# Layer norms and head norms: the power -1/2 on GpSimd in place of a root on ScalarE and a reciprocal on VectorE

## The chip, the cores and the metric

The kernel runs on one core of one Trainium2 chip. The time is device microseconds from the start to the end of one execution. The engines of a core work side by side and wait for each other by semaphores: TensorE (PE in the rows) multiplies, VectorE (DVE) and ScalarE (ACT) read and write both memories of the core, GpSimd (POOL) only the large one, and SyncE (SP) issues transfers. Each engine executes its own instructions strictly in order: one that waits holds everything behind it.

## What is computed

Four layers of a small transformer, each an attention and a feed-forward part, on 2048 rows of 128 features. Each of the eight parts is added to its input and normalised:

```python
def _layernorm(x, axis=-1, eps=1e-05):
    m = jnp.mean(x, axis=axis, keepdims=True)
    v = jnp.var(x, axis=axis, keepdims=True)
    return (x - m) / jnp.sqrt(v + eps)

x = _layernorm(x + _L0_attn_ref(x, ...), axis=-1)
x = _layernorm(x + _L0_ffn_ref(x, ...), axis=-1)
...
x = _layernorm(x + _L3_ffn_ref(x, ...), axis=-1)
```

The feed-forward part of layer 0 is itself a small transformer of depth 2 with local attention. It has a layer norm of its own and an L2 norm of each query and key head of 64 features:

```python
def l2norm(t):
    return t / jnp.clip(jnp.linalg.norm(t, axis=-1, keepdims=True), 1e-12)
q = l2norm(q) * qs
k = l2norm(k) * ksc
q, k = rotary_xpos(q, k)      # then scores (8 * q) k, softmax, values
...
h = (h - mu) / jnp.sqrt(var + 1e-05) * lg + lb
```

## The kernel before

The rows are held as four batches b of 512: 128 partitions by four quarters of 128 features. The parts of the reference are eight stages after a short Begin: Paired (attention of layer 0), Local (its feed-forward), Shifted (attention 1), Experts (feed-forward 1), Paired again (attention 2), Ternary (feed-forward 2), Clipped (attention 3) and Routed (feed-forward 3). Each stage is a class. Its `plan` is one list of steps, such as ("scores", 7) or ("fin", b), and `sequence` strings the plans together, with the head of one stage among the tail steps of the one before. Every engine goes through that one list and executes its own share of each step (`on_tensor`, `on_vector`, `on_scalar`, `on_gpsimd`, `on_sync`). So the order on an engine is the order of the list, whatever is ready. A stage's `parts` says how many signals each engine gives in a step; an engine without an entry does nothing in it.

The step "fin" of a batch is its layer norm. `normalise_vector` (L328 to L346) runs on VectorE: four bn_stats (L331), four bn_aggr (L336), the addition of epsilon to the four variances of each row (L339), then a wait for ScalarE, the reciprocal (L341) and four subtract-and-multiply operations (L344) that write the new activations XK. `normalise_scalar` (L349 to L351) is ScalarE's share, the root of a 128x4 tile. Shifted has the same as steps "ln" (L1190 to L1197, root L1317) and "fin" (L1202, L1205). Local has it twice, as "ln" and as "fin". Of such norms there are 40. Behind "fin" comes "turnx": TensorE transposes the new activations and ScalarE copies them to XT.

ScalarE's functions lie in tables, and the compiler puts an ACT_TABLE_LOAD in front of an activation whose function is not in the table that is loaded. In the attention stages ScalarE takes exponentials of scores (L739 in Paired, L1298 in Shifted), in Experts SiLU (L2070), in Local exponentials and GELU in turn. TensorE writes scores into the banks that those exponentials and VectorE's row maxima (L684 in Paired, L1147 and L1151 in Shifted) read.

Local's head norm is the step "norm", one for each of eight groups of four iterations. VectorE sums the squares (L1709), ScalarE takes the root of a 128x64 tile (L1811), VectorE takes the maximum with 1e-12 (L1714), the reciprocal (L1716) and eight times the query half (L1718). GpSimd then scales queries and keys in four "scale" steps (L1861, 128x1024 each) and has "sum" steps (L1856) between them. ScalarE's copies for the token shift (L1781, L1782) feed TensorE's products L1593.

In Routed a batch has nine "hidden" steps (L2725 and L2727 on TensorE, SiLU L2843, product L2815 on VectorE). GpSimd multiplies eight of the nine results by the routing weights ("scale", L2854), and "outward" is 72 matmuls (L2737) that wait for the batch's last scaling, followed by the addition (L2820) and "fin". The plan runs as follows:

```python
for n in range(9 * NB):
    b, c = n // 9, n % 9
    plan.append(("hidden", n))
    ...
    if b and c < 8:
        plan.append(("scale", b - 1, c))
    if n in (21, 29, 35):
        b = (21, 29, 35).index(n)
        plan += [("outward", b), ("fin", b)]
b = NB - 1
return plan + [("scale", b, c) for c in range(8)] + [("outward", b), ("fin", b)]
```

Of the kernel before, what the change touches and what calls it, by code (L numbers as in the profile page):

```python
# [41 lines left out]
def _tables():  # L42
# [17 lines left out]
    c["rqa"], c["rqb"], c["rka"], c["rkb"] = tile(ca * s2), tile(sa * s2), tile(ca / s2), tile(sa / s2)  # L60
# [267 lines left out]
def normalise_vector(e, w, vs, ss, key, y, st, dst):  # L328
# [532 lines left out]
class Shifted:  # L861
# [12 lines left out]
    def __init__(self, C):  # L874
# [2187 lines left out]
```

## Time and profile before

| | |
|---|---|
| runs | 2252.64 us median of 3 (2249.35 to 2254.05) |
| profiled execution, first to last instruction | 2256.5 us |
| TensorE busy | 2015.2 us, 89% |
| VectorE busy | 1461.1 us, 65% |
| ScalarE busy | 1170.8 us, 52% |
| GpSimd busy | 811.4 us, 36% |

The profiled execution has a span 3.9 us above the median of the runs. A timeline row gives the start and the length of an instruction, or of a run of equal ones, and in brackets how long the engine stood before it and what ended that. Groups give a mean over all instructions of a line and shape. A row of windows gives the busy time of each engine in a stretch and, as PEclk, the granted clock of TensorE as a share of full speed. TensorE being the busiest engine does not make it the bound everywhere: each stretch has to be read by what TensorE waits for in it.

### The profile page before, as it was taken

The page shows a single profiled execution, that of the slowest core. Times are in us where ns is not written, and L with a number is a line of the kernel's source. Part 1 is how long each engine was busy: PE and PEld are TensorE (multiplying, and loading weights), DVE is VectorE, ACT ScalarE, POOL GpSimd, SP SyncE. Part 2 cuts the span into 40 slices and gives each one's busy share as a digit, 9 for nine tenths or more (in the row PEclk, how much of TensorE's full clock was granted, in tenths as well). Part 3 has the DMA queues.
Part 4 walks back from the last instruction along what each step waited for, and adds up shares of the span by engine and source line. Part 5 has one row for each costly group of instructions (what it writes and reads, how often), then busy time and mean ns, then how long its engine had stood idle before and what let it go on. Part 6 is the DMA issues. An engine that isn't in the chain of part 4 may idle for free.

```text
span 2256.5 us, 44998 instructions
## 1 busy us (share of the span) xinstructions
PE 2015.2 (89%) x17759; PEld 1190.8 (53%) x17759; DVE 1461.1 (65%) x2920; ACT 1170.8 (52%) x1950; POOL 811.4 (36%) x1153
## 2 busy tenths in 40 slices
PE   7887789999878999998999889999799898999888
PEld 3343456666644454544665344444565665666446
DVE  5775677888778777773555776121677676767474
ACT  2565456656623454555332467332576675757432
POOL 4554333433127748342001321000545344453042
PEclk8999899999998999999999899999999999999999
DMA  3430111111234434210201220000465564655161
GB/s 124 140 111 2 25 32 27 30 32 28 64 108 128 131 91 138 75 34 14 91 1 62 84 84 19 33 0 1 156 208 173 176 207 133 207 175 168 50 127 45
DMA packets 183993, 199.15 MB, mean 88 GB/s; under 512 B 55922, under 2 KB 152486, under 8 KB 179302
## 3 DMA queue, kind: packets, MB, share of 16 engines
q1 hardware_dynamic: 183782, 196.27, 29.6%
q8 instruction: 141, 2.31, 0.4%
q14 instruction: 70, 0.57, 0.1%
HBM read 93.53 MB, written 92.08 MB: 82 GB/s over the span
## 4 chain that ended last, share of the span: by engine, by line
PE 35%; DVE 7%; ACT 6%; issue 2%; DMA 2%; POOL 1%; SPq 1%; DVEq 0%; ACTq 0%; POOLq 0%
PE PS L2134 5%; PE PS L357 4%; PE PS L2383 3%; PE PS L2399 3%; PE PS L2371 3%; PE PS L1985 3%; ACT AR L2543 3%; PE PS L1972 2%; PE PS L1975 2%; PE PS L2737 2%; PE PS L617 1%; PE PS L2725 1%; PE PS L2727 1%; PE PS L596 1%; PE PS L2143 1%
## 5 line engine op out<-in xcount | busy, mean ns | idle before, releaser
L1298 ACT ACTIVATE AR<-PS 128x1024 f32<-128x1024 f32 x160 | 162.5, 1023 | 122.5 <-PE PS L1047 121.6
L739 ACT ACTIVATE AR<-PS 128x1024 f32<-128x1024 f32 x160 | 162.6, 1024 | 92.4 <-PE PS L548 44.5
L1151 DVE TENSOR_REDUCE AR<-PS 128x2 f32<-128x768 f32 (+1 forms) x192 | 159.9, 864 | 52.1 <-PE PS L1026 29.9
L2599 POOL TENSOR_TENSOR RA<-AR,RA 128x288 f32<-128x288 f32 x128 | 88.1, 697 | 275.3 <-DVE RA L2475 141.0
L2543 ACT ACTIVATE AR<-PS,AR 128x512 f32<-128x512 f32 x256 | 173.7, 686 | 23.6 <-DVE AR L2464 23.4
L2464 DVE TENSOR_REDUCE AR<-PS 128x2 f32<-128x1024 f32 x128 | 156.7, 1225 | 12.9
L2371 PE MATMUL PS<-AR 64*128 64x200 f32 (+2 forms) x1280 | 145.9, 352 | 3.5 <-ACT AR L2543 3.5
L1856 POOL TENSOR_TENSOR AR<-AR 128x1024 f32<-128x1024 f32 x32 | 75.4, 2356 | 176.8 <-DVE AR L1704 176.8
L2383 PEld LDWEIGHTS PS<-CC,AR 64*128 64x128 f32 x2048 | 77.4, 140 | 98.3 <-issue 76.5
L2383 PE MATMUL PS<-CC,AR 64*128 64x64 f32 x2048 | 92.0, 229 | 38.9 <-DVE AR L2470 11.5
L2371 PEld LDWEIGHTS PS<-AR 64*128 64x128 f32 x1280 | 110.4, 192 | 7.1 <-ACT AR L2543 3.2
L2134 PE MATMUL PS<-AR,RA 128*128 128x512 f32 x256 | 110.2, 592 | 0.0
L1593 PE MATMUL PS<-RA,AR 128*128 128x512 f32 x192 | 98.9, 626 | 6.1 <-ACT AR L1782 6.1
L617 PE MATMUL PS<-AR 128*32 128x512 f32 (+3 forms) x1024 | 100.3, 467 | 4.1 <-POOL AR L802 2.8
L1375 POOL TENSOR_SCALAR_AFFINE_SELECT AR<-AR 128x512 f32<-128x512 f32 (+1 forms) x128 | 72.3, 567 | 53.0 <-ACT AR L1298 52.7
L1060 PE MATMUL PS<-AR 128*32 128x128 f32 (+3 forms) x1024 | 87.3, 448 | 4.3 <-POOL AR L1378 3.8
L679 DVE TENSOR_REDUCE AR<-PS 128x2 f32<-128x1024 f32 x64 | 77.5, 1221 | 20.6 <-PE PS L578 19.9
L2070 ACT ACTIVATE AR<-PS 128x512 f32<-128x512 f32 x64 | 37.8, 597 | 102.1 <-PE PS L1972 98.7
L573 PE MATMUL PS<-AR 48*128 48x512 bf16 (+7 forms) x512 | 67.1, 324 | 21.5 <-ACT AR L739 12.8
L681 DVE TENSOR_REDUCE AR<-PS 128x2 f32<-128x768 f32 x64 | 61.2, 956 | 37.4 <-PE PS L578 37.1
L2551 ACT ACTIVATE RA<-PS 128x512 f32<-128x512 f32 x96 | 53.7, 596 | 60.6 <-PE PS L2383 60.6
L2551 ACT ACTIVATE AR<-PS 128x512 f32<-128x512 f32 x96 | 54.4, 602 | 56.0 <-PE PS L2383 56.0
(370 smaller groups left out, 5043.8 us busy)
## 6 DMA issues: line engine op xcount, KB each, us to landing
ZD<-RC SPq DMA_DIRECT2D x32, 1152.0 KB
AR<-ZD SPq DMA_DIRECT2D x32, 640.0 KB
ZP<-AR SPq DMA_DIRECT2D x128, 160.0 KB, 2.8
SP<-AR SPq DMA_DIRECT2D x40, 384.0 KB, 2.6
AR<-SP SPq DMA_DIRECT2D x128, 96.0 KB
RA<-SP SPq DMA_DIRECT2D x32, 384.0 KB
SP<-AR SPq DMA_DIRECT2D x40, 256.0 KB, 2.9
RC<-RC SPq DMA_DIRECT2D x64, 130.0 KB
```

What stands on the lines that cost most here:

```text
L357: i = e.matmul(o[g:g + 64], x[:, g:g + 64], y, **how)
L617: i = e.matmul(b6[32 * j:32 * j + 32, 128 * kb:512], self.VP[b % 2][:, 16 * kb + 4 * (k % 4) + j, :], self.PT[at % 6][:, r, a:a + wd], sta ...
L739: e.activation(self.PT[m % 6], C.PS[:, 2 * s:2 * s + 2, :], ACT.Exp).then_inc(S["s_turned"].sem, 1)
L1151: i = e.tensor_reduce(nm[:, :, 4 * up + q:4 * up + q + 1], src[:, :, a:a + wd], AX, ALU.max, negate=True)
L1298: e.activation(self.PT[m % 6], C.PS[:, 2 * s:2 * s + 2, :], ACT.Exp).then_inc(S["s_turned"].sem, 1)
L1593: e.matmul(o, self.HT[:, L % NB, 64 + 128 * q:192 + 128 * q], W["wqkv" + str(L // NB)][:, 512 * x:512 * x + 512], start=True, stop=True).t ...
L2134: m = e.matmul(ba, w4[:, k, 128 * c:128 * c + 128], src[:, k, :], start=k == 0, stop=k == 3)
L2371: i = e.matmul(C.bank[2 * (n % 2) + hh][:, lo:hi], self.QT[p % 2][h, 128 * q:128 * q + 128], src[p % 2][h, lo:hi], start=True, stop=True)
L2383: i = e.transpose(both[x][:, 64 * a:64 * a + 64], self.PP[n % 5][h, a // 4, 16 + 128 * (a % 4):144 + 128 * (a % 4)], C.ident[h, h])
L2464: e.tensor_reduce(self.NMX[n % 4], s, AX, ALU.max, negate=True).then_inc(S["v_scores"].sem, 1)
L2543: i = e.activation(self.PP[n % 5][:, hh, 16:528], C.bank[2 * (n % 2) + hh], ACT.Exp, bias=self.NMX[n % 4][:, hh:hh + 1], accum_out=self.DE ...
L2551: e.activation(self.turned(n, g), o.rearrange("p (a j) -> p a j", a=8), ACT.Copy).then_inc(S["s_backs"].sem, 1)
```

## The change

The root on ScalarE and the reciprocal on VectorE become one operation of GpSimd, a tensor_tensor with the operation power and a constant -0.5 that is written once, in Begin, into a column of the statistics tile. The constant's step "pad" gets the name C.half, for which every user waits. GpSimd so gets a share in every "fin" and "ln", at the place that these have in the plan. In "norm" the maximum moves to GpSimd too (of the square, with 1e-24), the factor 8 goes into the constant tables by which the queries are multiplied later, and neither ScalarE nor VectorE has a share in the step any more. "norm" and "ln" of Local are otherwise at their old places in the plan.

```diff
-    c["rqa"], c["rqb"], c["rka"], c["rkb"] = tile(ca * s2), tile(sa * s2), tile(ca / s2), tile(sa / s2)
+    c["rqa"], c["rqb"], c["rka"], c["rkb"] = 8 * tile(ca * s2), 8 * tile(sa * s2), tile(ca / s2), tile(sa / s2)
...
-def normalise_vector(e, w, vs, ss, key, y, st, dst):
+def normalise_vector(e, w, vs, gs, key, y, st, dst):
...
     e.tensor_scalar_add(st[:, 32:36], st[:, 25:32:2], 1e-5).then_inc(vs.sem, 1)
-    w.wait_ge(ss, *key)
-    e.reciprocal(st[:, 40:44], st[:, 36:40]).then_inc(vs.sem, 1)
-    w.wait_ge(vs, *key, part=at + 4)
+    w.wait_ge(gs, *key)
     for q in range(NT):
         i = e.tensor_scalar(dst[:, 128 * q:128 * q + 128], y[:, 128 * q:128 * q + 128],
-                            st[:, 24 + 2 * q:25 + 2 * q], st[:, 40 + q:41 + q], ALU.subtract, ALU.mult)
+                            st[:, 24 + 2 * q:25 + 2 * q], st[:, 36 + q:37 + q], ALU.subtract, ALU.mult)
     i.then_inc(vs.sem, 1)
 
-def normalise_scalar(e, w, vs, ss, key, st):
-    w.wait_ge(vs, *key, part=vs.per - 2)
-    e.activation(st[:, 36:40], st[:, 32:36], ACT.Sqrt).then_inc(ss.sem, 1)
+def normalise_gpsimd(e, C, w, vs, gs, key, st):
+    w.wait_ge(C.half)
+    w.wait_ge(vs, *key, part=vs.per - 1)
+    e.tensor_tensor(st[:, 36:40], st[:, 32:36], C.ST[:, 0, 44:45].broadcast_to((128, 4)), ALU.pow).then_inc(gs.sem, 1)
...
         if step[0] == "pad":
+            e.memset(C.ST[:, 0, 44:45], -0.5)
...
-        elif kind == "norm":
-            L = n
-            SM, vn = self.SM[L % 3], S["v_norm"]
-            w.wait_ge(S["s_norm"], L)
-            e.tensor_scalar(SM[:, :, 0:16], SM[:, :, 0:16], 1e-12, None, ALU.max).then_inc(vn.sem, 1)
-            w.wait_ge(vn, L, part=1)
-            e.reciprocal(SM[:, :, 16:32], SM[:, :, 0:16]).then_inc(vn.sem, 1)
-            w.wait_ge(vn, L, part=2)
-            e.tensor_scalar(SM[:, :, 16:24], SM[:, :, 16:24], 8.0, None, ALU.mult).then_inc(vn.sem, 1)
...
-        elif kind == "norm":
-            SM = self.SM[n % 3]
-            w.wait_ge(S["v_sum"], 4 * n + 3)
-            e.activation(SM[:, :, 0:16], SM[:, :, 0:16], ACT.Sqrt).then_inc(S["s_norm"].sem, 1)
...
+        elif kind == "norm":
+            SM, gn = self.SM[n % 3], S["g_norm"]
+            w.wait_ge(C.half)
+            w.wait_ge(S["v_sum"], 4 * n + 3)
+            e.tensor_scalar(SM[:, :, 0:16], SM[:, :, 0:16], 1e-24, None, ALU.max).then_inc(gn.sem, 1)
+            w.wait_ge(gn, n, part=1)
+            e.tensor_tensor(SM[:, :, 16:32], SM[:, :, 0:16], C.ST[:, 0:1, 44:45].broadcast_to((128, 4, 16)), ALU.pow).then_inc(gn.sem, 1)
+        elif kind == "ln":
+            normalise_gpsimd(e, C, w, S["v_ln"], S["g_ln"], step[1:], self.LN[n % 2])
...
     def on_gpsimd(self, e, w, step):
-        S = self.S
+        C, S = self.C, self.S
+        if step[0] == "fin":
+            normalise_gpsimd(e, C, w, S["v_fin"], S["g_fin"], step[1:], C.ST[:, step[1] % 2, :])
+            return
```

The other stages get the same calls. ScalarE's queue has 117 ACT_TABLE_LOADs before and 48 after.

ScalarE in Shifted, around the layer norm of the first batch; L1298 is the exponential, L1303 a copy, L1317 the root, L1321 the copy to XT. Before:

```order
L1303 ACTIVATE AR<-PS 128x512 [waits t_group,t_piece]
L1298 ACTIVATE AR<-PS 128x1024 [waits t_turned]
L1317 ACT_TABLE_LOAD
L1317 ACTIVATE ST<-ST 128x4 [waits v_ln]
L1298 ACT_TABLE_LOAD
L1298 ACTIVATE AR<-PS 128x1024 [waits t_turned]
L1292 ACTIVATE AR<-PS 48x128 [waits t_flip,y_out]
```

and after, with the lines of the changed kernel (L1297 the exponential, L1302 the copy):

```order
L1302 ACTIVATE AR<-PS 128x512 [waits t_group,t_piece]
L1297 ACTIVATE AR<-PS 128x1024 [waits t_turned] x2
L1291 ACTIVATE AR<-PS 48x128 [waits t_flip,y_out]
L1297 ACTIVATE AR<-PS 128x1024 [waits t_turned]
L1297 ACTIVATE AR<-PS 128x1024 [waits t_turned,t_group]
```

The root and both table loads are gone, and the exponentials follow each other.

GpSimd in Local, around the head norm and layer norm of one group of four; L1856 (after: L1839) is "sum", L1861 (L1855) "scale". Before:

```order
L1866 TENSOR_TENSOR AR<-AR,RA 128x512 [waits y_out,v_out]
L1856 TENSOR_TENSOR AR<-AR 128x1024 [waits v_lin]
L1861 TENSOR_TENSOR AR<-AR 128x1024 [waits g_sum,v_norm]
L1856 TENSOR_TENSOR AR<-AR 128x1024 [waits v_lin]
L1861 TENSOR_TENSOR AR<-AR 128x1024 [waits g_sum]
```

and after:

```order
L1860 TENSOR_TENSOR AR<-AR,RA 128x512 [waits y_out,v_out]
L1839 TENSOR_TENSOR AR<-AR 128x1024 [waits v_lin]
L1844 TENSOR_SCALAR AR<-AR 128x4x16 [waits v_sum]
L1846 TENSOR_TENSOR AR<-AR,ST 128x4x16 [waits g_norm]
L350 TENSOR_TENSOR AR<-AR,ST 128x4 [waits v_ln]
L1855 TENSOR_TENSOR AR<-AR 128x1024 [waits g_sum,g_norm]
```

Maximum (L1844), power (L1846) and the layer norm's power (L350), which waits for VectorE's variance, stand ahead of the first scaling.

GpSimd in Routed, from the stage's start to the end of the program; L2854 (after: L2851) is "scale", eight for each batch. Before:

```order
L2854 TENSOR_TENSOR AR<-AR 128x512 [waits v_hidden] x7
L2854 TENSOR_TENSOR AR<-AR 128x512 [waits v_hidden,y_fetch1]
L2854 TENSOR_TENSOR AR<-AR 128x512 [waits v_hidden] x7
L2854 TENSOR_TENSOR AR<-AR 128x512 [waits v_hidden,y_fetch0]
L2854 TENSOR_TENSOR AR<-AR 128x512 [waits v_hidden] x7
L2854 TENSOR_TENSOR AR<-AR 128x512 [waits v_hidden,y_fetch1]
L2854 TENSOR_TENSOR AR<-AR 128x512 [waits v_hidden] x7
L281 UNCONDITIONAL_BRANCH
```

and after:

```order
L2851 TENSOR_TENSOR AR<-AR 128x512 [waits v_hidden] x3
L350 TENSOR_TENSOR ST<-ST 128x4 [waits v_fin]
L2851 TENSOR_TENSOR AR<-AR 128x512 [waits v_hidden] x4
L2851 TENSOR_TENSOR AR<-AR 128x512 [waits v_hidden,y_fetch0]
L2851 TENSOR_TENSOR AR<-AR 128x512 [waits v_hidden] x2
L350 TENSOR_TENSOR ST<-ST 128x4 [waits v_fin]
L2851 TENSOR_TENSOR AR<-AR 128x512 [waits v_hidden] x5
L350 TENSOR_TENSOR ST<-ST 128x4 [waits v_fin]
L2851 TENSOR_TENSOR AR<-AR 128x512 [waits v_hidden,y_fetch1]
L2851 TENSOR_TENSOR AR<-AR 128x512 [waits v_hidden] x7
L350 TENSOR_TENSOR ST<-ST 128x4 [waits v_fin]
```

The power of the first three batches now stands between scalings, each behind VectorE's variance of its batch; the fourth batch's eight scalings come after the third power.

## Rows read from the trace of the kernel before

**Rows 1.** page, part 1: busy us and share of the span, by engine

```profile
PE 2015.2 (89%) x17759; PEld 1190.8 (53%) x17759; DVE 1461.1 (65%) x2920; ACT 1170.8 (52%) x1950; POOL 811.4 (36%) x1153
```

**Rows 2.** waits: engine, what for, us in total, times, longest us

```profile
ACT ST L351 <- DVE ST L339: 124.1, 25, 14.0
```

**Rows 3.** groups by line and form, ScalarE: line, op, count | busy us, mean ns

```profile
L351 ACT ACT_TABLE_LOAD x26 | 33.4, 1283 | 0.5
```

**Rows 4.** timeline of ScalarE, Shifted: start us, us, engine, line, op, tiles, count

```profile
820.80 1.28 ACT L1317 ACT_TABLE_LOAD   x1
823.06 0.20 ACT L1317 ACTIVATE ST<-ST 128x4 f32<-128x4 f32 x1 [0.98 <-DVE ST L1197]
...
824.58 1.02 ACT L1298 ACTIVATE AR<-PS 128x1024 f32<-128x1024 f32 x1
```

**Rows 5.** the same of TensorE, Shifted; in brackets idle us before and releaser

```profile
825.65 0.45 PE L1023 MATMUL PS<-AR,RA 96*128 96x512 bf16 x1 [2.39 <-ACT AR L1298]
```

**Rows 6.** timeline of VectorE, Paired, the first batch's norm

```profile
129.83 1.22 DVE L684 TENSOR_REDUCE AR<-PS 128x4 f32<-128x1024 f32 x1
```

**Rows 7.** timeline of TensorE, the same place

```profile
130.95 0.61 PE L573 MATMUL PS<-AR 48*128 48x512 bf16 x2 [3.11 <-ACT AR L739]
...
132.64 0.61 PE L596 MATMUL PS<-AR 51*128 51x256 bf16 x4
```

**Rows 8.** timeline of VectorE, Experts

```profile
1098.02 1.12 DVE L344 TENSOR_SCALAR XK<-YB,ST 128x128 f32<-128x128 f32 x4
1099.78 1.29 DVE L2039 TENSOR_TENSOR AR<-PS,AR 128x512 f32<-128x512 f32 x2 [0.65 <-ACT AR L2070]
```

**Rows 9.** timeline of TensorE, Experts

```profile
1100.53 1.72 PE L1985 MATMUL PS<-RC,AR 128*128 128x128 f32 x13 [2.24 <-DVE AR L2039]
```

**Rows 10.** windows: us; PE, PEld, DVE, ACT, POOL busy; PEclk, DMA share, GB/s

```profile
129.00:137.00 8.00, 6.05 (x46) 2.43 (x46) 4.79 (x8) 5.62 (x7) 1.91 (x3) 0.57 0.57 178
1341.00:1349.00 8.00, 7.24 (x55) 3.00 (x55) 4.16 (x4) 4.76 (x6) 0.00 (x0) 0.57 0.20 56
1098.00:1105.00 7.00, 4.76 (x24) 3.04 (x24) 4.19 (x11) 2.76 (x4) 0.00 (x0) 1.00 0.00 0
```

**Rows 11.** groups by line and form, GpSimd

```profile
L1349 POOL TENSOR_TENSOR AR<-AR 128x512 f32<-128x512 f32 x21 | 24.3, 1156 | 1.9
...
L1363 POOL TENSOR_TENSOR AR<-AR 128x16 f32<-128x16 f32 x16 | 3.5, 218 | 1.3
```

**Rows 12.** timeline of ScalarE, Local, one group of four

```profile
416.03 0.26 ACT L1811 ACTIVATE AR<-AR 128x64 f32<-128x64 f32 x1 [1.62 <-DVE AR L1709]
```

**Rows 13.** timeline of GpSimd, Local

```profile
417.40 1.90 POOL L1861 TENSOR_TENSOR AR<-AR 128x1024 f32<-128x1024 f32 x1 [7.17 <-DVE AR L1718]
```

**Rows 14.** timeline of TensorE, Local

```profile
417.42 1.99 PE L1593 MATMUL PS<-RA,AR 128*128 128x512 f32 x4 [1.21 <-ACT AR L1782]
```

**Rows 15.** groups by line and form, VectorE

```profile
L339 DVE TENSOR_SCALAR ST<-ST 128x4 f32<-128x4 f32 x28 | 5.8, 207 | 1.0
...
L339 DVE TENSOR_SCALAR AR<-AR 128x4 f32<-128x4 f32 x8 | 5.0, 628 | 0.3
```

**Rows 16.** timeline of VectorE, Local

```profile
418.55 0.78 DVE L339 TENSOR_SCALAR AR<-AR 128x4 f32<-128x4 f32 x1
```

**Rows 17.** timeline of GpSimd, Routed

```profile
2227.72 6.17 POOL L2854 TENSOR_TENSOR AR<-AR 128x512 f32<-128x512 f32 x5 [11.10 <-DVE AR L2815]
```

**Rows 18.** timeline of VectorE, Routed

```profile
2224.60 0.17 DVE L339 TENSOR_SCALAR ST<-ST 128x4 f32<-128x4 f32 x1
...
2242.94 0.17 DVE L339 TENSOR_SCALAR ST<-ST 128x4 f32<-128x4 f32 x1
```

**Rows 19.** timeline of TensorE, Routed

```profile
2190.66 10.08 PE L2737 MATMUL PS<-RC,AR 128*128 128x128 f32 x72
...
2232.65 8.20 PE L2737 MATMUL PS<-RC,AR 128*128 128x128 f32 x72
2241.64 8.31 PE L2737 MATMUL PS<-RC,AR 128*128 128x128 f32 x72 [0.78 <-DVE YB L2820]
```

More of the change, by code:

```diff
@@ L385, in __init__ @@
         self.S = C.flags(self.plan, self.parts)
+        C.half = self.S["v_pad"]
         self.load = {n: C.flag("load_" + n, [()], 96 if n in ("b", "c", "rc") else 16) for n in ("x", "cc", "cb", "a", "b", "c", "rb", "rc", "rd")}
@@ L463, in __init__ @@
             "t": {"lin": 1, "scores": 1, "rows": 1, "turned": 1, "group": 1, "value": 1, "piece": 1, "proj": 2, "turnx": 1},
-            "v": {"lin": 1, "sa": 1, "first": 1, "scores": 1, "value": 1, "piece": 2, "proj": 1, "fin": 5},
-            "s": {"sa": 1, "first": 1, "rows": 1, "turned": 1, "take": 1, "proj": 1, "fin": 1, "turnx": 1},
-            "g": {"init": 3, "sb": 4, "rows": 4, "turned": 1, "proj": 1},
+            "v": {"lin": 1, "sa": 1, "first": 1, "scores": 1, "value": 1, "piece": 2, "proj": 1, "fin": 4},
+            "s": {"sa": 1, "first": 1, "rows": 1, "turned": 1, "take": 1, "proj": 1, "turnx": 1},
+            "g": {"init": 3, "sb": 4, "rows": 4, "turned": 1, "proj": 1, "fin": 1},
         }
@@ L808, in on_gpsimd @@
                             self.bo.unsqueeze(1).broadcast_to((128, 4, 128)), ALU.add).then_inc(S["g_proj"].sem, 1)
+        elif kind == "fin":
+            normalise_gpsimd(e, C, w, S["v_fin"], S["g_fin"], key, C.ST[:, key[0] % 2, :])
     def on_sync(self, e, w, step):
@@ L909, in __init__ @@
             "v": {"init": 1, "lk": 1, "ls": 1, "lw": 1, "lu": 1, "sa": 1, "beside": 4, "scores": 1, "rows": 2, "value": 1, "first": 1,
-                  "piece": 4, "proj": 1, "ln": 3, "fin": 2},
-            "s": {"sa": 1, "flip": 1, "turned": 1, "take": 1, "first": 1, "ot": 1, "ln": 1, "turnx": 1},
-            "g": {"tabs": 2, "vals": 2, "lw": 1, "sb": 4, "rows": 4, "turned": 1, "proj": 1},
+                  "piece": 4, "proj": 1, "ln": 3, "fin": 1},
+            "s": {"sa": 1, "flip": 1, "turned": 1, "take": 1, "first": 1, "ot": 1, "turnx": 1},
+            "g": {"tabs": 2, "vals": 2, "lw": 1, "sb": 4, "rows": 4, "turned": 1, "proj": 1, "ln": 1},
         }
@@ L1457, in __init__ @@
             "t": {"lin": 1, "v": 1, "turnq": 1, "turnk": 1, "scores": 1, "flip": 1, "av": 1, "ot": 1, "out": 1, "two": 1, "hg": 1, "ha": 1, "four": 1, "five": 1, "turnx": 1, "fill": 1},
-            "v": {"init": 1, "lin": 1, "sum": 1, "norm": 3, "turnk": 1, "soft": 2, "av": 2, "out": 1, "ln": 5, "two": 1, "ha": 1,
-                  "four": 1, "add": 1, "fin": 5},
-            "s": {"shift": 1, "square": 1, "v": 1, "norm": 1, "turnq": 1, "exp": 1, "flip": 1, "ot": 1, "ln": 1,
-                  "hg": 1, "five": 1, "fin": 1, "turnx": 1},
-            "g": {"init": 1, "tabs": 1, "sum": 1, "scale": 1, "four": 1},
+            "v": {"init": 1, "lin": 1, "sum": 1, "turnk": 1, "soft": 2, "av": 2, "out": 1, "ln": 4, "two": 1, "ha": 1,
+                  "four": 1, "add": 1, "fin": 4},
+            "s": {"shift": 1, "square": 1, "v": 1, "turnq": 1, "exp": 1, "flip": 1, "ot": 1,
+                  "hg": 1, "five": 1, "turnx": 1},
+            "g": {"init": 1, "tabs": 1, "sum": 1, "norm": 2, "scale": 1, "ln": 1, "four": 1, "fin": 1},
         }
@@ L1927, in __init__ @@
             "t": {"gate1": 1, "hidden": 2, "outward": 1, "turnx": 1},
[L1928 to L1929 removed]
+            "v": {"gate1": 2, "gate2": 3, "gate3": 6, "hidden": 1, "outward": 4, "fin": 4},
+            "s": {"gate2": 1, "hidden": 1, "turnx": 1},
+            "g": {"fin": 1},
         }
@@ L2077, in on_scalar, with on_gpsimd @@
             e.activation(C.XT[:, b, 0:512], C.bank[7], ACT.Copy).then_inc(S["s_turnx"].sem, 1)
+    def on_gpsimd(self, e, w, step):
+        C, S, key = self.C, self.S, step[1:]
+        normalise_gpsimd(e, C, w, S["v_fin"], S["g_fin"], key, C.ST[:, key[0] % 2, :])
 class Ternary:
@@ L2201, in on_scalar, with on_gpsimd @@
             e.activation(C.XT[:, b, 0:512], C.bank[6], ACT.Copy).then_inc(S["s_turnx"].sem, 1)
+    def on_gpsimd(self, e, w, step):
+        C, S, key = self.C, self.S, step[1:]
+        normalise_gpsimd(e, C, w, S["v_fin"], S["g_fin"], key, C.ST[:, key[0] % 2, :])
 class Clipped:
@@ L2607, in on_gpsimd @@
                 i.then_inc(S["g_wo"].sem, 4)
+        elif kind == "fin":
+            normalise_gpsimd(e, C, w, S["v_fin"], S["g_fin"], key, C.ST[:, key[0] % 2, :])
     def on_sync(self, e, w, step):
@@ L2669, in __init__ @@
             "t": {"gate1": 1, "gate6": 1, "hidden": 2, "outward": 1},
[3 rows of a table removed]
+            "v": {"gate2": 5, "gate3": 7, "gate4": 6, "gate5": 3, "hidden": 1, "outward": 1, "fin": 4},
+            "s": {"gate1": 1, "gate6": 1, "hidden": 1},
+            "g": {"scale": 1, "fin": 1},
         }
```

70 lines of the change are left out of this document (26 added, 44 removed), and 3 rows, old and new, of the table cv.

## The prediction

> **What bounds the kernel now.** I read the page first: TensorE is busy 2015.2 of 2256.5 us, ScalarE 1170.8, GpSimd 811.4 [rows 1]. A change that touches only ScalarE, VectorE and GpSimd can therefore move the end only where TensorE stands still, or where its clock is low after it stood still. The waits view names the place to look: ScalarE stood 124.1 us in 25 waits on the variance of a layer norm [rows 2]. In front of the square root it reloads its function table, 26 loads of 1283 ns on that line alone [rows 3], and again after it for the next exponential or SiLU. So I read the timelines around the norms and asked at each one which wait of TensorE ends last, then the granted clock behind it, and then the order of GpSimd's queue, because the new operation has to stand in it.
>
> **What is removed.** In an attention stage ScalarE loads the root's table ahead of time at 820.80, waits in order for the variance until 823.06, loads back, and the next exponential starts at 824.58 [rows 4]. Its scores were there at about 820.8. TensorE has no free bank and stands 2.39 us until 825.65 [rows 5]. Without root and loads that exponential runs at 820.8 and the one behind it right after; what is late next is VectorE's maximum of the scores, within about 0.4 us. I take 2.0 of the 2.39 us: 3 places, **6.0 us**. In the Paired stages the gap is longer, 3.11 us, but behind it stand a row maximum (L684, from 129.83, 1.22 us long) that VectorE takes only after the norm [rows 6, 7]; the transposes of the norm's result, ahead of it in TensorE's order, wait for the norm too. The maximum keeps its time (129.83 moves by the length of the removed reciprocal at most), so the matmuls at 132.64 can come at 130.9: 1.7 us. Two places of this kind and two with a gap half as long, at 1.0: **5.4 us**. In Experts SiLU no longer waits for the table. VectorE's last scaling ends at 1099.14, its product (L2039) then starts at 1099.1 instead of 1099.78, and the chain before it is shorter by the reciprocal: 0.9 of the 2.24 us [rows 8, 9]. Four places, and two more of the same form at the ends of Experts and in Ternary: **5.4 us**. In Clipped, VectorE's own chain is what TensorE waits for; three places at 0.2 give **0.6 us**. Sum of the gaps: 17.4 us.
>
> **The clock behind the gaps.** After such a gap the granted clock falls to half, 1.2 GHz in place of 2.4. Over 129 to 137 the mean is 0.57, and the same over 1341 to 1349; that is 8 x 0.43 = 3.4 us of full speed lost each time, with TensorE busy 6.05 and 7.24 of the 8 us [rows 10]. Seven such stretches follow gaps that the root makes, three of 3.4 us and four of half that, 17.0 us together. Gaps of 2.24 us and more were mostly followed by it, though not always: 1098 to 1105 kept 1.00 [rows 9, 10]. The shortened gaps (0.4 to 1.4 us) should mostly keep the clock. Bounds 0 and 17; I take 11, since some stretches will be caught again and some of the lost speed is hidden behind ScalarE. Both together: **28 us** off the path, by bounds 9 (half of the gaps) and 34.
>
> **The price of the power.** No row shows it. The nearest are plain GpSimd operations on two tensors: 218 ns for 16 elements a partition, 1156 for 512 [rows 11], that is about 0.19 us fixed and 1.9 ns an element. Below: 0.2 us for the 4 elements of a layer norm and 0.3 for the 64 of a head norm, as cheap as an addition. Above: 100 times the slope, 0.9 and 12 us, a function worked out step by step. I take ten times the slope: 0.27 us for 4, 1.4 us for 64, because a power is more work than an addition and nothing in the rows says how much more. At 0.27 the root's place in the chain (0.20 us of ScalarE and the reciprocal behind it [rows 4]) is filled almost evenly; the chain is some 0.2 us shorter, which is in the terms above. The constant of -1/2 costs nothing: one memset at the start, under the first loads.
>
> **Local stage.** Here the head norm moves too. Now its root starts at 416.03 and GpSimd's first scaling (L1861) at 417.40 [rows 12, 13]: 1.4 us, against 0.2 for the maximum plus 1.4 for the power. ScalarE's shift copies (the 1.21 us gap of TensorE before 417.42 [rows 14]) no longer stand behind the root, and VectorE is spared three short operations. Against that, the power of the layer norm comes ahead of L1861 in GpSimd's queue, and the applying operations on VectorE (L344) then run beside L1861. What that does is seen now: the addition of epsilon on 4 elements takes 207 ns on average in the layer norms at stage ends, but 628 ns in Local [rows 15], and the one at 418.55 took 0.78 us [rows 16] and ended when L1861 did [rows 13]. So VectorE would be held to about 419.8 again and end its norm near 420.9, where it ends now. Bounds -12 us (1.5 in each of 8 groups) and, at the upper price, far above; I take 0. The Trainium skill, GPSIMD Engine Reference, section 1 (Specifications), says the same against this change: GpSimd shares its SBUF interfaces with VectorE, in contention with a 2-port mode or with two SBUF inputs of VectorE. By that rule the 12 us stay away, without it they come; the trace agrees, with 628 against 207 ns.
>
> **Routed stage: a wait is added.** GpSimd executes its steps in the order of the plan, and the fourth batch's eight scalings (L2854) stand behind the third batch's norm. Now GpSimd has nothing in the norm and does them early: the last five run 2227.72 to 2233.89 [rows 17]. Afterwards the power of the third batch heads the queue, and its variance is there only at 2243.11 [rows 18]. Then come 8 x 1.23 us (6.17 over 5 [rows 17]) = 9.9 us of scalings, until 2243.1 + 0.3 + 9.9 = 2253.3. The last 72 matmuls wait for the last of them; today they start at 2241.64 [rows 19]. That is **+11.7 us** at the very end of the kernel, where nothing hides it. TensorE stands some 12 us before them; the same 72 matmuls took 10.08 us at 2190.66 after a stand, and 8.31 at 2241.64 [rows 19], so **+1.8 us** more. The same move at the first two norms costs nothing: at the second, the variance is there at 2224.77 [rows 18], the five scalings behind it end near 2225.0 + 6.2 = 2231.2, and their matmuls start at 2232.65 [rows 19]; the first has only four behind it. In Clipped a norm's power stands ahead of GpSimd's copies of the next pair, which come later by it; what hides them is the previous pair's scores and exponentials, since the copies feed only transfers that are wanted behind those. I take nothing; if that cover is gone, TensorE waits for them there.
>
> **Sum.** -17.4 - 11 + 0 + 11.7 + 1.8 = -14.9, less about 1 us for delays of GpSimd's masks behind the power in Shifted: **-14 us**, against the profiled span of 2256.5. That span lies 3.9 us above the median of the runs; I take the difference over to the median: 2252.6 - 14 = 2238.6, say 2239.
>
> **Rivals.** (1) The power is dear on GpSimd. For: nothing shows its price. Against: GpSimd is busy only 36% of the span [rows 1]. With e us an element, the layer norms lose 4e in some 20 places where VectorE's chain ends last, and each of the 8 head norms 64e less the 1.1 us that it has spare. The 14 us are used up at 80e + 8(64e - 1.1) = 14, e = 0.039 us, twenty times the slope of an addition; at 0.06 the time is 2239 + 27 = 2266, slower than before. (2) The gains are given back: VectorE's chain or GpSimd's masks are late in place of the root, and the clock falls as before. Half of the gaps and 3 us of clock against 13.5 in Routed: 2252.6 - 8.7 - 3 + 13.5 = 2254. For it speaks that VectorE is busy 4.79 of 8 us where the clock is low [rows 10]. (3) All comes: 34 us off, and 6 of Local's 12, with Routed as above: 2226. (4) The power does not rid ScalarE of its reloads, since exponential, GELU and SiLU change places anyway. The order of the changed kernel has 48 loads for 117, so that would be a surprise; only Routed's 13.5 would stay: 2266.
>
> **How the numbers follow.** Forecast 0.50 (2230 to 2248), rival 1 0.20, rival 2 0.16, rival 3 0.12, rival 4 0.02. A measurement tells 0.2%, 4.5 us, from no change: faster is below 2248.1, slower above 2257.1. Faster: 0.46 of the forecast, all of rival 3: 0.58. Same: the rest of the forecast, most of rival 2, a little of rival 1: 0.19. Slower: 0.23. The range 2226 to 2266 leaves out the lower half of rival 3 and the dear half of rival 1.
>
> **What would show it.** In the changed profile: about 48 table loads; no gap of TensorE over 1 us before the exponential behind a Shifted norm; fewer stretches at half clock up to 1400 us; a row of about 0.27 us for the power of 4 and 1.4 for that of 64; L344 in Local lengthened beside L1855 (now L1861); and, in Routed, GpSimd's eight L2851 (now L2854) in one piece after the third norm, with TensorE idle for 12 us before its last 72 matmuls. The forecast is wrong if the power costs over 1 us for 4 elements, or if TensorE waits as long as before with VectorE as releaser.

## The result, and the profile after

The changed kernel takes 2364.3 us (median; 2363.0 to 2365.1, 4 runs), the one before 2253.35 beside it: ratio 1.050, 95% interval 1.048 to 1.052. That is 111 us slower, where 2239 us had been forecast, and outside the range. The profiled execution has a span of 2362.7 us.

On the page (part 1, and of part 2 the granted clock in 40 slices) TensorE has the same number of matmuls as before [rows 1]. It stands longer (2362.7 - 2032.2 = 330.5 us without a matmul, for 241.3 before), and its clock is low more often:

```profile
PE 2032.2 (86%) x17759; PEld 1210.4 (51%) x17759; DVE 1468.4 (62%) x2857; ACT 1076.1 (46%) x1833; POOL 939.3 (40%) x1209
...
PEclk8989889889998999999999899999999999999998
```

The operation of which no row was known before, by groups of line and form (line, engine, operation, tiles, count | busy us, mean ns | idle before): L1846 is the head norm's power, L350 and L1385 those of the layer norms, L1844 the head norm's maximum.

```profile
L1846 POOL TENSOR_TENSOR AR<-AR,ST 128x64 f32<-128x64 f32 x8 | 84.4, 10550 | 0.7
...
L350 POOL TENSOR_TENSOR ST<-ST 128x4 f32<-128x4 f32 x28 | 28.5, 1019 | 405.9 <-DVE ST L339 404.3 <-DMA ZM<-AR 1.5
...
L350 POOL TENSOR_TENSOR AR<-AR,ST 128x4 f32<-128x4 f32 x8 | 8.1, 1010 | 4.9 <-DVE AR L339 4.9
...
L1385 POOL TENSOR_TENSOR ST<-ST 128x4 f32<-128x4 f32 x4 | 4.1, 1021 | 28.6 <-DVE ST L1198 28.6
...
L1844 POOL TENSOR_SCALAR AR<-AR 128x64 f32<-128x64 f32 x8 | 3.0, 374 | 34.4 <-DVE AR L1709 34.4
```

A power of 128x4 takes 1.02 us, one of 128x64 10.55 us. Between the two lie 60 elements and 9.53 us: 0.159 us an element and 0.38 us fixed. The forecast had taken 0.019 and 0.19, from the additions of [rows 11].

To see where the time goes, the two traces are laid over each other at the starts of the norms' bn_stats (L331, and L1190 in Shifted). The fourth "fin" of each stage ends it. In us, of profiled executions:

| from norm to norm | before | after | difference |
|---|---|---|---|
| start to end of Paired | 220.1 | 219.0 | -1.1 |
| Local | 454.8 | 542.8 | +88.0 |
| Shifted | 386.0 | 378.4 | -7.6 |
| Experts | 176.4 | 174.1 | -2.3 |
| Paired, second | 189.8 | 189.5 | -0.3 |
| Ternary | 159.7 | 160.1 | +0.4 |
| Clipped | 558.0 | 564.0 | +6.0 |
| Routed | 106.0 | 128.6 | +22.6 |
| sum | 2250.7 | 2356.3 | +105.6 |

Each column is one profiled execution. Stages that a run does not change differ between profiles too: the second Paired stage takes 186.6 us in e8 below, 3.2 less than before, and Clipped 4.3 more. So +88.0, +22.6 and -7.6 are clear of that, and the smaller differences are not, nor all of Clipped's +6.0. Local and Routed hold the loss, and Shifted is the one stage that clearly gains. GpSimd in Local, timeline (start us, us, engine, line), one group of four iterations; it answers to [rows 13]:

```profile
454.15 0.37 POOL L1844 TENSOR_SCALAR AR<-AR 128x64 f32<-128x64 f32 x1 [5.86 <-DVE AR L1709]
454.61 10.55 POOL L1846 TENSOR_TENSOR AR<-AR,ST 128x64 f32<-128x64 f32 x1
465.12 1.01 POOL L350 TENSOR_TENSOR AR<-AR,ST 128x4 f32<-128x4 f32 x1
466.10 1.90 POOL L1855 TENSOR_TENSOR AR<-AR 128x1024 f32<-128x1024 f32 x1
```

VectorE and TensorE there, and the window behind (us; PE, PEld, DVE, ACT, POOL busy; PEclk, DMA share, GB/s); they answer to [rows 16] and [rows 14]:

```profile
455.29 0.17 DVE L339 TENSOR_SCALAR AR<-AR 128x4 f32<-128x4 f32 x1
466.17 2.68 DVE L342 TENSOR_SCALAR AR<-AR 128x128 f32<-128x128 f32 x4 [10.71 <-POOL AR L350]
```

```profile
470.86 2.31 PE L1599 MATMUL PS<-CC,AR 128*128 128x128 f32 x8 [12.50 <-ACT AR L1791]
```

```profile
460.00:476.00 16.00, 5.06 (x49) 4.37 (x49) 8.45 (x14) 3.72 (x6) 12.22 (x5) 0.57 0.07 17
```

The chain can be read off. The sum of squares is there at 454.1. GpSimd is in the power until 465.1. Behind it in its queue stand the layer norm's power, which VectorE has waited for since 455.5, and the first scaling of the group. VectorE stands 10.71 us, ScalarE then waits for VectorE, and TensorE stands 12.50 us. While it stands, its clock falls to half (1.2 GHz of 2.4), and it is still at half until 475.0, some 4 us after TensorE has gone on (mean 0.57 over 460 to 476): eight matmuls of L1599 take 2.31 us there, and 1.04 at 448.94. VectorE waits so in each of the eight groups, and in four of them TensorE stands the full 12.5 us. The waits view (who, for whom: us in total, times, longest us) sums it up:

```profile
DVE AR L342 <- POOL AR L350: 67.6, 8, 10.7
...
PE PS L1599 <- ACT AR L1791: 51.3, 8, 12.5
...
DVE XK L342 <- POOL ST L350: 36.1, 28, 3.3
```

In Shifted the gain is there as forecast. ScalarE, GpSimd and TensorE around the first norm, to be held against [rows 4] and [rows 5]:

```profile
908.40 2.10 ACT L1297 ACTIVATE AR<-PS 128x1024 f32<-128x1024 f32 x2
911.46 0.27 ACT L1291 ACTIVATE AR<-PS 48x128 bf16<-48x128 f32 x1 [0.95 <-PE PS L1034]
911.94 1.02 ACT L1297 ACTIVATE AR<-PS 128x1024 f32<-128x1024 f32 x1 [0.21 <-PE PS L1048]
```

```profile
911.74 1.02 POOL L1385 TENSOR_TENSOR ST<-ST 128x4 f32<-128x4 f32 x1 [1.49 <-DVE ST L1198]
```

```profile
912.84 0.60 PE L1048 MATMUL PS<-RA 99*128 99x512 bf16 x2 [0.38 <-DVE AR L1152]
```

No table load stands among the exponentials. The power of 1.02 us runs beside them, while VectorE takes two row maxima before it applies the norm, and in place of TensorE's gap of 2.39 us there is one of 0.38 us.

### The profile page after: what moved, and what is told of

Read it like the earlier page. It is cut to its first block, busy times and chain, and to the rows that moved or that the text cites. A ratio compares the mean times of both kernels' runs of the same rounds, so it can differ in the third digit from the quotient of the medians.

```text
span 2362.7 us, 44886 instructions
## 1 busy us (share of the span) xinstructions
PE 2032.2 (86%) x17759; PEld 1210.4 (51%) x17759; DVE 1468.4 (62%) x2857; ACT 1076.1 (46%) x1833; POOL 939.3 (40%) x1209
## 3 DMA queue, kind: packets, MB, share of 16 engines
q8 instruction: 141, 2.31, 0.4%
## 4 chain that ended last, share of the span: by engine, by line
PE 31%; issue 6%; DVE 5%; ACT 4%; POOL 3%; DMA 2%; SPq 1%; DVEq 0%; POOLq 0%; ACTq 0%
PE PS L2131 5%; PE PS L2381 3%; PE PS L356 3%; PE PS L2397 3%; PE PS L2369 3%; ACT AR L2541 2%; PE PS L1980 2%; PE PS L1967 2%; PE PS L1970 2%; PE PS L618 1%; PE PS L2722 1%; PE PS L2724 1%; DVE AR L2462 1%; DVE XK L342 1%; PE PS L2734 1%
## 5 line engine op out<-in xcount | busy, mean ns | idle before, releaser
L1297 ACT ACTIVATE AR<-PS 128x1024 f32<-128x1024 f32 x160 | 162.6, 1024 | 123.1 <-PE PS L1048 122.0
L350 POOL TENSOR_TENSOR ST<-ST 128x4 f32<-128x4 f32 x28 | 28.5, 1019 | 405.9 <-DVE ST L339 404.3
L2462 DVE TENSOR_REDUCE AR<-PS 128x2 f32<-128x1024 f32 x128 | 156.8, 1225 | 13.3 <-DVE PS L2459 0.5
L1839 POOL TENSOR_TENSOR AR<-AR 128x1024 f32<-128x1024 f32 x32 | 75.4, 2356 | 162.7 <-DVE AR L1704 162.7
L1599 PE MATMUL PS<-CC,AR 128*128 128x128 f32 x256 | 43.1, 314 | 75.3 <-ACT AR L1791 51.3
L1846 POOL TENSOR_TENSOR AR<-AR,ST 128x64 f32<-128x64 f32 x8 | 84.4, 10550 | 0.7
```

Of the source, the lines that this page charges most:

```text
L1297: e.activation(self.PT[m % 6], C.PS[:, 2 * s:2 * s + 2, :], ACT.Exp).then_inc(S["s_turned"].sem, 1)
L2462: e.tensor_reduce(self.NMX[n % 4], s, AX, ALU.max, negate=True).then_inc(S["v_scores"].sem, 1)
```

## Experiments

Two theories stood against each other: (A) the length of the power; (B) the new place in GpSimd's queue, whatever the operation there costs. Later came (C), that VectorE is slowed while GpSimd's operations run beside it, and (D), latency against total time of GpSimd in Local. Times are medians; the kernel before ran on the same chip beside each. They came in three batches: e1 to e4 on one chip, e5 to e8 and e9 to e11 on a second. The kernel before took 2254.0, 2255.1 and 2252.2 us in them, so a difference of 3 us between runs of different batches tells nothing.

### A cheap operation in the power's place

```diff
-    e.tensor_tensor(st[:, 36:40], st[:, 32:36], C.ST[:, 0, 44:45].broadcast_to((128, 4)), ALU.pow).then_inc(gs.sem, 1)
+    e.tensor_scalar(st[:, 36:40], st[:, 32:36], 0.0, 0.02, ALU.mult, ALU.add).then_inc(gs.sem, 1)
```

The same is done in Shifted's "ln" and in Local's "norm". The inverse root is thus left out; order and waits stay.

> Every power on GpSimd (head norms and layer norms) is replaced by one cheap GpSimd operation of the same shape at the same place, which writes the constant 0.02; the inverse root is left out, all waits stay. Theory A, the length of the power is what went wrong (10.55 us for 64 elements, 1.02 us for 4): the time falls from 2364 to about the forecast, 2230 to 2250, and Local is no longer than before. Theory B, the new place in GpSimd's queue is what costs (power of the layer norm and head norm ahead of the scalings, whatever their length): Local keeps 40 us or more of its 86, the time stays above 2290.

Measured (e1): 2241.6 us (2238.8 to 2258.9, 10 runs) beside 2254.0 of before, ratio 0.9955 (0.9937 to 0.9973). The groups on GpSimd:

```profile
L350 POOL TENSOR_SCALAR ST<-ST 128x4 f32<-128x4 f32 x28 | 5.4, 193 | 401.3 <-DVE ST L339 399.5 <-DMA ZM<-AR 1.5
...
L1846 POOL TENSOR_SCALAR AR<-AR 128x64 f32<-128x64 f32 x8 | 2.0, 245 | 0.7
```

At these prices the kernel comes within 3 us of the forecast. That flatters the forecast somewhat: it had 1.4 us for the 64 elements, and this operation takes 0.25, so at the forecast's own price the kernel could be up to 8 x 1.15 = 9 us longer, by an estimate that puts all of it on the path. Local is 5.7 us shorter than before in place of 88 longer, with the same order in every queue. Theory A holds; the queue order alone (B) costs nothing in Local on balance.

> Only the 128x64 power of Local's eight head norms is replaced by a cheap constant operation, the 40 powers of 128x4 stay. Theory A: eight times 10.55 - 0.4 = 81 us fall away almost whole, 2364 to about 2280, and against the run with everything cheap the 128x4 powers cost 25 to 40 us (40 x 0.8 us, less where hidden). Theory B: less than 40 us fall away.

Here only the head norm's power is replaced. Measured (e2): 2288.05 us (ratio 1.016, 1.014 to 1.018). The eight powers of 128x64 are thus worth 76 us, and the 40 of 128x4 46 us (2288.05 - 2241.6). That is more than the 25 to 40 expected, and more than the 40 x 0.83 = 33 us by which they are longer. The stages share it: 16.0 us in Local, 5 or so in each of both Paireds, Shifted and Experts, 6.3 in Routed.

### The head norm as before, the layer norms by the power

The diff is that of the head norm, undone: root (ScalarE), maximum, reciprocal, factor (VectorE), tables without the 8.

> The head norm goes back to root on ScalarE, maximum, reciprocal and factor on VectorE; all layer norms keep the power on GpSimd. Theory A: Local loses its 86 us but for the layer norms' 1 us, time about 2278 to 2290, that is still 1 to 2% above before, since Routed's tail (+22) and the 1 us powers eat what Shifted gains. Theory B: the layer norm's power ahead of the scalings still holds up Local, time over 2300.

Measured (e3): 2293.1 us (ratio 1.018, 1.016 to 1.019), 3 us above the range expected. Local is 71.8 us shorter than in the changed kernel, but still 16.2 longer than before. That is more than the price of its twelve powers of 128x4 (eight in "ln" and four in "fin", 1 us each); e9 below takes most of the rest away.

### Local's queue: one long power or four short ones

```diff
             plan.append(("sum", n))
-            if n % 4 == 3:
-                plan.append(("norm", n // 4))
+            plan.append(("norm", n))
...
-            w.wait_ge(S["v_sum"], 4 * n + 3)
+            w.wait_ge(S["v_sum"], n)
```

Maximum and power then work on 128x16, and each scaling waits for its own quarter.

> As the changed kernel, but the head norm's maximum and power are done quarter by quarter (128x16 after each of the four sums) in place of 128x64 at the end of a group; the same elements in all. By 1.02 us for 4 elements and 10.55 for 64 one of 16 should take 0.38 + 16 x 0.159 = 2.9 us. Theory D, what costs in Local is that the first scaling of a group stands behind the whole power: three quarters then hide behind other work, 10.7 us a group become 2 to 3, and the time falls by 60 to 70, to about 2300. Rival, GpSimd's total time in Local is the bound: the total of 4 x 2.9 = 11.7 us a group is longer than 10.55, and the time does not fall, 2360 to 2370.

Measured (e6): 2306.3 us (ratio 1.024, 1.021 to 1.028), 58 us under the changed kernel where 60 to 70 were expected. The group of the power:

```profile
L1845 POOL TENSOR_TENSOR AR<-AR,ST 128x16 f32<-128x16 f32 x32 | 93.6, 2925 | 2.7
```

2.93 us for 16 elements, where the line through 4 and 64 gives 2.92: the price is linear. GpSimd now spends 93.6 us on powers in place of 84.4, and Local is 61.3 us shorter (481.5 for 542.8). So it is the serial stretch behind the last sum of squares that costs, not GpSimd's total time (theory D). One quarter of it, and the layer norm's power, are left in the chain, and TensorE stands 4.75 us in place of 12.50:

```profile
439.02 2.32 PE L1598 MATMUL PS<-CC,AR 128*128 128x128 f32 x8 [4.75 <-ACT AR L1790]
```

In both traces TensorE's wait leads back over ScalarE and VectorE to the layer norm's power (L350), which stands behind the head norm's in GpSimd's queue. Whether it would be enough to put the layer norm's power ahead of the head norm's was not tried.

### Routed: order and contention

```diff
+            if n == 35:
+                plan += [("scale", NB - 1, c) for c in range(8)]
             if n in (21, 29, 35):
...
-        return plan + [("scale", b, c) for c in range(8)] + [("outward", b), ("fin", b)]
+        return plan + [("outward", b), ("fin", b)]
```

> As the changed kernel, but in Routed the fourth batch's eight scalings stand in the plan ahead of the third batch's outward and norm; only GpSimd's order changes. If the scalings behind the power are what lengthens the end, the last 72 matmuls follow the ones before at once and 13 to 15 us fall away: 2350. If the end is long for another reason (the clock, the 1 us power in the last chain), under 4 us.

Measured (e4): 2344.9 us, 19.4 under the changed kernel, more than the 13 to 15 expected. In the changed kernel GpSimd and TensorE at the end are, to be held against [rows 17] and [rows 19],

```profile
2334.83 1.01 POOL L350 TENSOR_TENSOR ST<-ST 128x4 f32<-128x4 f32 x1 [14.44 <-DVE ST L339]
2335.81 9.81 POOL L2851 TENSOR_TENSOR AR<-AR 128x512 f32<-128x512 f32 x8
```

```profile
2345.76 9.78 PE L2734 MATMUL PS<-RC,AR 128*128 128x128 f32 x72 [13.26 <-POOL AR L2851]
```

and with the scalings ahead of the third norm TensorE is

```profile
2317.74 7.87 PE L2736 MATMUL PS<-RC,AR 128*128 128x128 f32 x69
2326.39 8.30 PE L2736 MATMUL PS<-RC,AR 128*128 128x128 f32 x72 [0.78 <-DVE YB L2819]
```

The gap of 13.26 us is 0.78 us, and the 72 matmuls take 8.30 us in place of 9.78. These two are 14.0 of the 15.0 us by which Routed is shorter (113.6 for 128.6). The other 4 to 6 us (by medians or by spans) are differences in the stages ahead, where nothing was changed, and between executions.

> All powers replaced by a cheap constant operation (the inverse root is left out) and Routed's order as in e4. If the +13.5 us of the end in Routed were a term of its own, as the forecast's sum had it, this run is 13 to 20 us under the one with cheap operations alone (2241.6): 2222 to 2229. If the end is hidden there or paid elsewhere, less than 5.

The same order with the cheap operation (e7, the inverse root left out): 2230.55 us (ratio 0.990, 0.988 to 0.993), 11 us under e1 by the medians, 14.1 by the spans (2237.1 and 2223.0), and 13.2 in Routed alone (108.5 for 121.7). The forecast had 13.5 for this term. The upper bound expected of this run, 2229, is missed by 1.5 us.

What was left in Routed is at the first two norms, which the forecast had taken at nothing. VectorE and TensorE in the changed kernel behind the variance of Routed's first batch:

```profile
2287.60 4.95 DVE L342 TENSOR_SCALAR XK<-YB,ST 128x128 f32<-128x128 f32 x4 [1.12 <-POOL ST L350]
```

```profile
2293.20 1.12 PE L2724 MATMUL PS<-XT,RC 128*128 128x512 f32 x2 [2.96 <-DVE AR L2812]
```

The four applying operations take 4.95 us; before they took 1.12. Seven scalings of 1.23 us run on GpSimd right then (8.62 us from 2287.53), since they had queued up behind the power. The products behind them are late, and TensorE stands 2.96 us. To test that, GpSimd was made to wait:

```diff
             normalise_gpsimd(e, C, w, S["v_fin"], S["g_fin"], step[1:], C.ST[:, step[1] % 2, :])
+            w.wait_ge(S["v_fin"], step[1])
             return
```

> As e4 (fourth batch's scalings ahead of the third norm), and in Routed GpSimd waits, behind each power, until VectorE has applied that norm, before it goes on with the scalings. Theory C: Routed's first two norms cost 3.2 and 4.9 us because VectorE's four applying operations run beside GpSimd's scalings and take 4.95 us in place of 1.11; with the wait they take about 1.1 again, TensorE's 2.3 us wait for VectorE is gone, and 5 to 7 us fall away against e4 (2344.9): 2338 to 2340, although a wait was added. Rival: the 1.02 us power and the later start are what costs; then the added wait only delays the scalings and the time is 2345 to 2350.

Measured (e5): 2341.0 us, 3.8 under e4 (2344.9) by the medians. That is less than expected and not clear of noise: the ratios to before are 1.041 (1.040 to 1.043) and 1.039 (1.036 to 1.042). The traces show it nevertheless: Routed is 5.5 us shorter (108.1 for 113.6). VectorE's L342 at Routed's second norm in e4 and in e5:

```profile
2305.72 4.95 DVE L342 TENSOR_SCALAR XK<-YB,ST 128x128 f32<-128x128 f32 x4 [1.12 <-POOL ST L350]
```

```profile
2307.26 1.12 DVE L342 TENSOR_SCALAR XK<-YB,ST 128x128 f32<-128x128 f32 x4 [1.12 <-POOL ST L350]
```

4.95 us beside the scalings, 1.12 without them. The stretch from the second norm to the third falls from 23.3 to 19.2 us, and before it was 18.3. A wait more made the stage faster. The same in Local, on e3:

```diff
             normalise_gpsimd(e, C, w, S["v_ln"], S["g_ln"], step[1:], self.LN[n % 2])
+            w.wait_ge(S["v_ln"], n)
```

> As e3 (head norm by root and reciprocal, layer norms by the power), and in Local GpSimd waits, behind the power of each layer norm, until VectorE has applied it, before it goes on with the scaling L1861. In e3 the four applying operations took 2.69 us beside that scaling (421.24 to 423.93) and TensorE then stood 2.90 us. Theory C (VectorE is held by GpSimd's running operation): they take 1.1 us, 1.6 us fall away in each of Local's groups, 8 to 15 us together, 2278 to 2285 against 2293. Rival: the scaling that now starts 1.1 us later is itself wanted; then nothing is gained, 2290 to 2300.

Measured (e9): 2280.7 us, 12.4 under e3, with ratios to before of 1.018 (1.016 to 1.019) and 1.012 (1.010 to 1.015). Local falls from 471.0 to 458.8 us, 4 us above before. VectorE's L342 and TensorE's next wait in e3, then in e9:

```profile
421.24 2.69 DVE L342 TENSOR_SCALAR AR<-AR 128x128 f32<-128x128 f32 x4 [1.13 <-POOL AR L350]
```

```profile
425.88 0.66 PE L1599 MATMUL PS<-CC,AR 128*128 128x128 f32 x4 [2.90 <-ACT AR L1800]
```

```profile
417.21 1.12 DVE L342 TENSOR_SCALAR AR<-AR 128x128 f32<-128x128 f32 x4 [1.13 <-POOL AR L350]
```

```profile
420.45 0.63 PE L1599 MATMUL PS<-CC,AR 128*128 128x128 f32 x4 [1.51 <-POOL AR L1862]
```

The applying operations take 1.12 us in place of 2.69, and the gap of TensorE is 1.51 us in place of 2.90.

### Only where the power is hidden

The kernel before, with Shifted's four norms alone changed (the part of the diff in Shifted, the constant, and a semaphore that is shared by name with a step of Local).

> The kernel before with the power on GpSimd in Shifted's four layer norms alone; all other norms keep root and reciprocal. In the changed kernel the stretch from the first to the fourth of these norms was 9.4 us shorter than before, with the true power of 1.02 us, because the exponentials no longer stand behind two table loads. If that holds alone: 2254 - 9 = 2244 to 2247, faster than before. If it was a shift of work from the longer Local stage, within 2 us of before.

Measured (e8): 2245.7 us (10 runs), ratio 0.996 (0.9948 to 0.9973).

> e8 once more beside e10 on the same chip, for the difference of the two: 2244 to 2247, ratio to before 0.995 to 0.998.

Measured (e11, the same kernel as e8): 2245.8 us (12 runs), ratio 0.9964 (0.9952 to 0.9975). Shifted is 9.9 and 9.7 us shorter than before (376.1 in e8 and 376.3 in e11 for 386.0). ScalarE and TensorE around the first norm, in e8:

```profile
820.36 1.02 ACT L1299 ACTIVATE AR<-PS 128x1024 f32<-128x1024 f32 x1 [0.21 <-PE PS L1050]
821.96 1.02 ACT L1299 ACTIVATE AR<-PS 128x1024 f32<-128x1024 f32 x1 [0.58 <-PE PS L1050]
```

```profile
821.26 0.61 PE L1050 MATMUL PS<-RA 99*128 99x512 bf16 x2 [0.39 <-DVE AR L1154]
```

The exponentials stand close together here too, and TensorE's 2.39 us gap is 0.39. In e8 the clock stays at full from 701 to 1025 us. Before, it fell to half behind each of the first three norms, for 3.4, 3.4 and 6.8 us, which costs 1.7 + 1.7 + 3.4 = 6.8 us of full speed; this part of the gain was forecast too.

> As e8 (power in Shifted's norms alone), and the power in the four norms of Experts too. The forecast gave 0.9 us a norm at a price of 0.27 us; the true power is 0.75 us longer, which leaves 0.15 us a norm: within 2 us of e8, 2244 to 2248. If VectorE's chain there has slack that the forecast did not see, 3 us or more faster than e8; if GpSimd's round trip costs more than its row, slower than e8.

Measured (e10, Experts' four norms changed as well): 2245.5 us, ratio 0.9966 (0.9949 to 0.9984): no difference to e11. Experts itself takes 174.1 us, and 174.3 and 176.0 in e8 and e11, where it is as before. In Experts the true price uses up the gain. VectorE and TensorE there in the changed kernel, to be held against [rows 8] and [rows 9]:

```profile
1175.87 1.12 DVE L342 TENSOR_SCALAR XK<-YB,ST 128x128 f32<-128x128 f32 x4 [1.22 <-POOL ST L350]
1176.90 1.28 DVE L2034 TENSOR_TENSOR AR<-PS,AR 128x512 f32<-128x512 f32 x2
```

```profile
1177.64 2.73 PE L1980 MATMUL PS<-RC,AR 128*128 128x128 f32 x13 [2.24 <-DVE AR L2034]
```

VectorE's product now starts right behind the norm, so SiLU is late no longer, but the norm ends later by the power, and TensorE's gap is 2.24 us as before. With the cheap operation (e1) the same gap is

```profile
1073.73 1.49 PE L1980 MATMUL PS<-RC,AR 128*128 128x128 f32 x11 [1.43 <-DVE AR L2034]
```

1.43 us, which is 0.8 less where 0.9 had been forecast.

## Why the forecast was wrong

**The price of the power** is the step that failed. The forecast bounded it by plain additions: 0.2 to 0.9 us for 4 elements, 0.3 to 12 for 64, and took 0.27 and 1.4, ten times the slope. Measured: 1.02 and 10.55, 84 times the slope. "Over 1 us for 4 elements" was the forecast's own sign of being wrong, and it came. The upper ends had been written down almost right, for the 4 elements too low by 0.1 us. What failed is the choice between them, and then the range, which reached only to 0.06 us an element (2266) though the bound named above was 0.19. With bounds 40 times apart and no row between, "a power is more work than an addition" was no reason for the low end, and rival 1 had far too little of the chance.

**Rival 1** is what came. Its mechanism holds. Its point of decision (0.039 us an element) was not tested closely; 0.159 lies far above it. By its formula 0.159 us gives 80 x 0.159 + 8 x (64 x 0.159 - 1.1) = 85 us, so 2324. Measured 2364. Of the missing 40, by estimates, the higher fixed part accounts for some 5 us (28 places at 0.19 us) and Routed's first two norms for 8. Local lost 88 us, 11.0 a group, where the formula gave 9.1 a group, 15 us in all. Two things are seen there that the formula lacks: the clock, still at half for some 4 us behind a stand of TensorE, and VectorE held up by the scaling, which in e3 was worth 12 us (e9). How the 15 us divide between them was not measured. The last 12 us are spread over the stages and were not followed up.

**The gaps and the clock** were right in mechanism, at about the price they were worked out for: e1 reaches 2241.6 for 2239. That the two are so close is in part luck, since e1's operation on 64 elements is cheaper than the 1.4 us of the forecast, and what the forecast missed goes both ways there (5.7 us gained in Local, 4.2 + 2.5 us lost at Routed's first two norms). Before Routed it is 35 us ahead, for 28 forecast: 13.3 in Shifted (forecast 6.0 and a share of the clock's 11), 8.0 in Experts, 5.0 and 5.2 in the Paired stages, 5.7 in Local (forecast 0). At the true price these gains go where VectorE's chain is what TensorE waits for, since each norm takes 0.75 us more: Experts gains 2.3 in place of 8.0 (and not even that clearly, by e8), the first Paired stage 1.1 in place of 5.0, the second 0.3 in place of 5.2. More than half is left in Shifted alone (7.6), where VectorE has other work between the variance and the applying.

**Routed's end** was right in mechanism and size: +11.7 and +1.8 forecast; the last of the four norms comes 13.95 us later than before against the third. The 72 matmuls took 9.78 us, not 8.31. e4 takes it away by order alone.

**Routed's first two norms** were taken at nothing, and cost 4.9 and 3.2 us against before. The price of the power is the smaller part of it, since they cost 4.2 and 2.5 us in e1 too. The forecast asked only whether the scalings would end in time, and not what they would do to VectorE while they ran. It had that very effect in hand: L339 at 628 in place of 207 ns in Local [rows 15], used there and not in Routed. The Trainium skill, GPSIMD Engine Reference, section 1 (Specifications), says that GpSimd shares its SBUF interfaces with VectorE, in contention with VectorE's instructions in a 2-port mode or with two SBUF inputs. The traces agree that the two are in each other's way, with 4.95 us for L342 beside the scalings and 1.12 without. Which of the two cases L342 is, no run here shows, and beside the power it was not slowed (1.11 us in e6, below).

**Local, beside the price**: 0 was taken, since the applying operations would be held by L1861. They are (2.69 for 1.12 us in e3), so that term's mechanism is right. The 0 was a little too cautious when the power is cheap (5.7 us gained) and too bright when it is not.

**Clipped** was forecast at -0.6 and is +6.0. This stays open in part. In e8 and e10, where nothing in Clipped is changed, it is 562.3 us and so 4.3 longer than in the profile of before; so a part of the 6 may be variation. The trace shows another part. GpSimd's copies behind the power now run beside the applying operations of three norms, which take 1.81 us where they took 1.11, so 2.1 us together:

```profile
1847.77 1.81 DVE L342 TENSOR_SCALAR XK<-YB,ST 128x128 f32<-128x128 f32 x4 [1.15 <-POOL ST L350]
```

The forecast had these copies in view and asked only whether they would be late. No run keeps them apart.

## What to carry to other kernels

Before an operation is moved to an engine, one must know its price there, for the shape that it has. Where no row shows it, a range that spans a factor of 40 has to stay in the forecast, and the long end has to be followed through the queue, into the wait and into the clock behind it. An operation that an in-order queue has to wait for gathers the work behind it. That work then runs in one piece, beside whatever VectorE does next. Where that slows VectorE, it may pay to hold it back by a wait, as it did in e9.

## What the runs showed of the hardware

- GpSimd's power costs 0.38 us and 0.159 us an element of a partition, linear over 4, 16 and 64 elements (1.02, 2.93, 10.55 us). The cheap operation of e1, one input and constants, took 193 and 245 ns in the same shapes, the maximum (L1844) 374 ns.
- VectorE's four operations that scale 128x128 took 1.12 us alone, 2.69 us beside one 1.90 us operation on GpSimd, and 4.95 us beside scalings of 1.23 us: about the time of four of these. By groups, in the changed kernel (342 and 371 ns before):

```profile
L342 DVE TENSOR_SCALAR XK<-YB,ST 128x128 f32<-128x128 f32 x112 | 50.6, 514 | 36.1 <-POOL ST L350 36.1
...
L342 DVE TENSOR_SCALAR AR<-AR 128x128 f32<-128x128 f32 x32 | 18.3, 633 | 67.6 <-POOL AR L350 67.6
```

- Not every operation of GpSimd slows VectorE. In e6 the same four operations ran beside a power of 128x16 and took 1.11 us:

```profile
227.05 1.11 DVE L342 TENSOR_SCALAR XK<-YB,ST 128x128 f32<-128x128 f32 x4 [1.13 <-POOL ST L350]
```

```profile
227.33 2.93 POOL L1845 TENSOR_TENSOR AR<-AR,ST 128x16 f32<-128x16 f32 x1
```

- Nor is every operation of VectorE slowed. The addition of epsilon (L339) took 0.78 us beside the scaling [rows 16] and 0.17 in the changed kernel at 455.29, inside a power of 10.55 us. The four bn_stats in front of it took 0.87 us beside the scaling before (from 417.23), and 0.87 in e3 with GpSimd idle (from 418.62). The products L1703 and L1704, which read TensorE's results, took 0.42 us beside the scaling in e9 (from 418.84) and 0.41 behind it. Which property of an operation decides was not isolated.

- After a stand of 12.56 us TensorE's 72 matmuls at the end of e1 took 10.08 us, for 8.30 behind a stand of 0.78 us (e4). The clock was at half in the stand and until 2224.5:

```profile
2220.65 10.08 PE L2734 MATMUL PS<-RC,AR 128*128 128x128 f32 x72 [12.56 <-POOL AR L2851]
```
